# Projections of a decoder layer: tokens normalised ahead of v's eviction, and x1 kept by batches behind keys

## The reference

```python
# x, ctx: (128, 64, 128) = (S, N, D)
x = x + attn(layernorm(x))              # over s for each n: softmax(tanh(q k / sqrt(D))) x, one head
xn = layernorm(x)
q, k, v = xn @ Wq.T + bq, ctx @ Wk.T + bk, ctx @ Wv.T + bv   # over n for each s, 16 heads of 8
x = x + (softmax(q k^T * 8**-0.5) v) @ Wo.T
x = x + soft_moe(x)                     # 16 experts of 16 slots; softmax over tokens and over slots
```

## Time and profile before

| what | value |
|---|---|
| runs | 594.53, 594.87, 598.77 us (median 594.87) |
| the profiled execution | 592.56 us, of which the span on the engines is 590.8 |
| PE busy | 505.0 us (85%) |
| DVE, ACT, POOL busy | 389.9 (66%), 376.9 (64%), 293.8 us (50%) |
| mean share of the 16 DMA engines, SP's queue | 26.5% |
| mean granted TensorE clock | 0.945 |

### The profile page before, as it was taken

One profiled execution on the slowest core, in us unless ns is written; L12 is line 12 of the kernel. 1 busy time (PEld: TensorE's weight loads), 2 busy tenths in 40 slices (PEclk: granted clock), 3 DMA queues, 4 the chain that ended last, 5 costly groups with the idle time before them and its releaser, 6 DMA issues. The chain is left out here.

```text
span 590.8 us, 19858 instructions
## 1 busy us (share of the span) xinstructions
PE 505.0 (85%) x7708; PEld 357.8 (61%) x7708; DVE 389.9 (66%) x1081; ACT 376.9 (64%) x567; POOL 293.8 (50%) x399
## 2 busy tenths in 40 slices
PE   4878858889879999999983089999999976999995
PEld 2557645565346666666652045655655645999995
DVE  4477635769978889899724366666676521677774
ACT  3757824555668878787782358889888654544440
POOL 4234313465668687787402876798898422100000
PEclk9979978999989999999998589999999985999998
DMA  6642114551001110111110002232232231444553
GB/s 183 184 138 107 73 55 137 164 153 46 1 22 35 29 41 25 40 28 36 41 41 1 1 36 75 75 111 94 76 111 96 84 100 48 158 138 146 159 152 98
DMA packets 60737, 49.32 MB, mean 83 GB/s; under 512 B 15472, under 2 KB 50416, under 8 KB 60656
## 3 DMA queue, kind: packets, MB, share of 16 engines
q1 hardware_dynamic: 60656, 48.20, 26.5%
HBM read 30.87 MB, written 17.04 MB: 81 GB/s over the span
## 5 line engine op out<-in xcount | busy, mean ns | idle before, releaser
L587 DVE TENSOR_REDUCE c_mx<-ps 128x16 f32<-128x1024 f32 x64 | 78.0, 1219 | 14.2 <-PE ps L742 13.3
L541 POOL TENSOR_TENSOR c_k_bd<-c_k,w_mask 128x512 bf16<-128x512 f32 x80 | 83.5, 1069 | 1.2 <-DVE c_work L625 1.2
L664 ACT ACTIVATE c_work<-ps 128x2048 f32<-128x2048 f32 x32 | 60.0, 1874 | 27.2 <-PE ps L771 27.1
L1330 PE MATMUL ps<-w_w,h_bd 128*64 128x128 f32 x1024 | 71.8, 280 | 5.5 <-DVE o_slot_out L1282 5.5
L1330 PEld LDWEIGHTS ps<-w_w,h_bd 128*64 128x64 f32 x1024 | 63.5, 141 | 6.3 <-DVE o_slot_out L1282 6.3
L1274 ACT ACTIVATE h_bd<-hidden 32x512 f32 (+1 forms) x64 | 40.3, 629 | 41.1 <-PE ps L1330 40.5
L1306 DVE TENSOR_TENSOR o_slot_out<-ps,w_b 128x512 f32<-128x512 f32 x64 | 44.0, 687 | 21.3 <-PE ps L1330 20.9
L1091 ACT ACTIVATE e_slot_in<-ps 128x1024 f32<-128x1024 f32 x32 | 32.5, 1017 | 27.9 <-PE ps L1153 27.9
L1344 PE MATMUL ps<-o_slot_out,ctx_sb 128*64 128x129 f32 x512 | 41.8, 274 | 1.3 <-DMA ctx_sb<-combine_scratch 0.9
L674 ACT ACTIVATE c_q_bd<-x_all,w_mask 128x512 f32<-128x512 f32 x64 | 42.9, 719 | 0.0
L561 POOL COPY c_v_bd<-c_v 64x512 f32<-64x512 f32 x32 | 21.8, 682 | 35.4 <-PE ps L791 26.8
(11 more groups left out here) (162 smaller groups left out, 1169.3 us busy)
## 6 DMA issues: line engine op xcount, KB each, us to landing
x_all<-x_scratch SPq DMA_DIRECT2D x128, 64.0 KB, 2.3
combine_scratch<-e_comb SPq DMA_DIRECT2D x16, 512.0 KB, 2.7
ctx_sb<-combine_scratch SPq DMA_DIRECT2D x16, 512.0 KB, 3.2
x_sb<-in_x SPq DMA_DIRECT2D x16, 256.0 KB, 3.3
ctx_sb<-in_ctx SPq DMA_DIRECT2D x16, 256.0 KB, 3.2
x_scratch<-a_x SPq DMA_DIRECT2D x16, 256.0 KB, 2.0
e_rden<-dispatch_inverses SPq DMA_DIRECT2D x64, 64.0 KB, 2.0
out<-o_y SPq DMA_DIRECT2D x64, 64.0 KB, 2.1
```

Of the source, the lines that this page charges most:

```text
L541: ins = nc.gpsimd.tensor_tensor(k_bd[:, c.m2, s, :], k32[:, c.v, :], w["mask8"][:, s:s + 1].to_broadcast([P, TOK]), ALU.mult)
L587: nc.vector.reduce_max(mx[:, c.m2, :, p], ps[:, SCORE:SCORE + 2, :].rearrange("p a (h m) -> p (a h) m", m=N), AX_X).then_inc(mx_sb.sem, 1)
L664: nc.scalar.activation(prob[:, h, :], ps[:, 0:4, :].rearrange("p a b -> p (a b)"), ACT.Exp, scale=float(HD) ** -0.5).then_inc(p_sb.sem, 1)
L1330: ins = nc.tensor.matmul(ps[64 * (g % 2):64 * (g % 2) + 64, p, at:at + D], h_bd[:, c.m2, s % 2 * PC + s // 2, g].rearrange("p e k -> p (e ...
```

## The change

1. The scratch tensor x1 is laid out [N, S, D] instead of [S, N, D]. A store of stage 1 now has 512 pieces of 512 B instead of 128 of 2 KB.
2. A chunk's token at half a, column q is now s = 8c + 4a + q, so the four tokens of a partition lie next to each other in DRAM. The load of a chunk (in stage 2, and again in stage 3) is one transfer of 256 KB in 128 pieces of 2 KB instead of four of 64 KB in pieces of 512 B. On the DRAM side it runs over [2 halves][64 n][512 elements], on the SBUF side over [128 partitions][512 elements]. The semaphores count one landing instead of four; `k_at` and the index of `v_bd` follow.
3. DVE normalises chunk t+19 ahead of v(t+20)'s eviction instead of behind it.
4. The output of a chunk goes out by two transfers of 128 KB instead of four of 64 KB.

```diff
+    x1_tokens = x1_dram.rearrange("n s d -> s n d")
-                    sp.dma_start(x1_dram[:, bass.ts(c.v, BC), :], x1[:, c.m2]).then_inc(x1_out.of(c), 16)
+                    sp.dma_start(x1_tokens[:, bass.ts(c.v, BC), :], x1[:, c.m2]).then_inc(x1_out.of(c), 16)
...
-    x1_v = x1_dram.rearrange("(c u a r) n d -> c u a n r d", u=2, a=2, r=2)
+    x1_v = x1_dram.rearrange("n (c a p) d -> c a n (p d)", a=2, p=PC)
...
-                    for u in range(2):
-                        for a in range(2):
-                            sp.dma_start(x_all[N * a:N * (a + 1), c.v * PC + 2 * u:c.v * PC + 2 * u + 2, :], x1_v[c.v, u, a]).then_inc(x_in.of(c), 16)
+                    sp.dma_start(x_all[:, c.v * PC:(c.v + 1) * PC, :].rearrange("p q d -> p (q d)"), x1_v[c.v]).then_inc(x_in.of(c), 16)
...
-                            rows, q_at, k_at = slice(32 * T, 32 * (T + 1)), (4 * u + 2 * r + a) * N, (4 * u + 2 * a + r) * N
+                            rows, q_at, k_at = slice(32 * T, 32 * (T + 1)), (4 * u + 2 * r + a) * N, (4 * a + 2 * u + r) * N
...
-    out_v = out.rearrange("(c u a r) n d -> c u a n r d", u=2, a=2, r=2)
+    out_v = out.rearrange("(c a p) n d -> c a n p d", a=2, p=PC)
...
-                for u in range(2):
-                    for a in range(2):
-                        sp.dma_start(out_v[bass.ds(c.v, 1), u, a].rearrange("o n r d -> (o n) r d"),
-                                     y[N * a:N * (a + 1), c.m2, 2 * u:2 * u + 2, :]).then_inc(y_out.of(c), 16)
+                for a in range(2):
+                    sp.dma_start(out_v[bass.ds(c.v, 1), a].rearrange("o n p d -> (o n) p d"), y[N * a:N * (a + 1), c.m2]).then_inc(y_out.of(c), 16)
...
-        x1_dram = nc.dram_tensor("x1_scratch", [S, N, D], F32).ap()
+        x1_dram = nc.dram_tensor("x1_scratch", [N, S, D], F32).ap()
```

More of the change, by code:

```diff
@@ L463, in cross_attention @@
     zeroed, ps_zeroed, ones_set = kit.sem("c_zeroed"), kit.sem("c_ps_zeroed"), kit.sem("c_ones_set")
-    x_in = kit.landings("c_x_in", 4)
+    x_in = kit.landings("c_x_in")
     stat, rooted, normed = kit.sig("c_stat", 2), kit.sig("c_rooted", 2), kit.sig("c_normed")
@@ L470, in cross_attention @@
     k_bd_dve, k_bd_pool = kit.sig("c_k_bd_dve"), kit.sig("c_k_bd_pool")
-    x_again = kit.pairs("c_x_again", 4)
+    x_again = kit.pairs("c_x_again")
     sc_ps, mx_sb = kit.sig("c_sc_ps", 4), kit.sig("c_mx_sb", 4)
@@ L514, in _ @@
                     sp.wait_ge(q_bd_sb.sem, q_bd_sb.at(c))
-                    for u in range(2):
-                        for a in range(2):
-                            sp.dma_start(x_all[N * a:N * (a + 1), c.v * PC + 2 * u:c.v * PC + 2 * u + 2, :], x1_v[c.v, u, a]).then_inc(x_again.of(c), 16)
+                    sp.dma_start(x_all[:, c.v * PC:(c.v + 1) * PC, :].rearrange("p q d -> p (q d)"), x1_v[c.v]).then_inc(x_again.of(c), 16)
         @block.gpsimd
@@ L612, in _ @@
                     ins.then_inc(stat.sem, 1)
[L613 to L619, removed]
                 c = t.plus(LEAD_X + 2)
@@ L627, in _ @@
                     ins.then_inc(normed.sem, 1)
+                c = t.plus(LEAD_C)
+                if c:
+                    dve.wait_ge(v_ps.sem, v_ps.at(c))
+                    nc.vector.tensor_tensor(
+                        v_all[:, c.v * PC:(c.v + 1) * PC, :], ps[:, MISC, :].rearrange("p (a d) -> p a d", a=PC),
+                        w["bv"][:].rearrange("p (o d) -> p o d", o=1).to_broadcast([P, PC, D]),
+                        ALU.add).then_inc(v_sb.sem, 1)
                 c = t.plus(LEAD_X + 3)
@@ L740, in scores @@
                     for T in range(2):
-                        rows, q_at, k_at = slice(64 * T, 64 * (T + 1)), (4 * u + 2 * r + a) * N, (4 * u + 2 * a + r) * N
+                        rows, q_at, k_at = slice(64 * T, 64 * (T + 1)), (4 * u + 2 * r + a) * N, (4 * a + 2 * u + r) * N
                         ins = nc.tensor.matmul(ps[N * r:N * (r + 1), SCORE + T, :].rearrange("p (s m) -> p s m", s=8),
@@ L790, in values @@
                             to, of = (2 * T + a) * N, (8 * T + 4 * a + j) * N
-                            ins = nc.tensor.matmul(ps[32 * j:32 * j + 2 * V1, VALUE, to:to + N], v_bd[:, c.m2, 2 * u + a, 4 * T + j, :],
+                            ins = nc.tensor.matmul(ps[32 * j:32 * j + 2 * V1, VALUE, to:to + N], v_bd[:, c.m2, 2 * a + u, 4 * T + j, :],
                                                    prob[:, u, of:of + N], start=True, stop=True)
@@ L1239, in experts_out @@
     y_ps, den, y_sb = kit.sig("o_y_ps", 4), kit.sig("o_den", 2), kit.sig("o_y_sb", 2)
-    y_out = kit.landings("o_y_out", 4)
-    out_v = out.rearrange("(c u a r) n d -> c u a n r d", u=2, a=2, r=2)
+    y_out = kit.landings("o_y_out", 2)
+    out_v = out.rearrange("(c a p) n d -> c a n p d", a=2, p=PC)
     first, last, lo, hi = -2, CHUNKS, 2, CHUNKS - 2
```

## The result

The changed kernel takes 623.12 us (median of 4 runs, 621.48 to 626.66) against 594.7 us for the kernel before (4 runs, 593.04 to 598.77). The ratio is 1.047 with a 95% interval of 1.0431 to 1.0509: slower by 28 us. The profiled execution is the longest of its four, 626.66 us with a span of 624.9.

A forecast was written before the change was run, and what follows sets the result against it. Stage 2, bound by a loop through PE and DVE, would become bound by x1's loads on two engines: 592.56 + 32.8 - 0.4 + 1.0 + 0.4 - 1.6 = 624.8, with 1.2 added for typical runs 626 us, range 617 to 637.

The forecast's parts named there:

- Engines per load: Loads of x1: each transfer goes over two engines, because its DRAM side begins with a count of 2.
- sixteen-engine rivals: Loads of x1 get sixteen engines: 586 us with the order's gain, chance 0.13; 592.6 us without it, chance 0.04.
- Price of a load: Stage 2: 5.4 us a load on two engines, 6.3 us a chunk with context; last statistics 32.8 us later.
- Behind the last landing: End of stage 2: DVE's way from last landing to last normalising takes 4.2 us instead of 4.58, -0.4 us.
- The clock: Stage 2: PE's gaps lower its granted clock to 0.50, costing +1.0 us (0 to 3) at the stage's end.
- the rival of 636 us: Stage 2: PE at clock 0.50 becomes the bound with steps of 7.4 us, 636 us in all, chance 0.15.
- Stage 3: Second fetch of x1, also on two engines: 0 us; at worst PE pays 14 us.
- The stores: Stage 1: smaller pieces lengthen DVE's one wait for a store, +0.4 us (0 to 1.5).
- The tail: Output at the kernel's end: two issues a chunk instead of four, -1.6 us (-2.0 to -0.8).
- Part 3, 6.5 us if the tokens come in time: Stage 2: normalising ahead of v's eviction leaves a DVE and POOL loop of 3.4 us, PE's step 3.7, gain 6.5 us.
- the sixteen-engine rival's 586: Loads of x1 on sixteen engines, 0.7 us each, and the new DVE order gives its 6.5 us: 586 us, chance 0.13.
- The third rival: Sixteen engines, but POOL's masks, sharing its queue with the roots, close the loop at 4.2 us: 592.6 us, chance 0.04.

The follow-up runs named there:

- halves: The changed kernel with each load of x1, in stages 2 and 3, sent as two transfers of 64 rows: 591.55 us, ratio 0.9952 to the kernel before.
- cut62: halves with each half load of stage 2 cut into transfers of 62 and 2 rows: 622.93 us, ratio 1.0487 to the kernel before.
- cut61: halves with each half load of stage 2 cut into transfers of 61 and 3 rows: 700.73 us in one run.
- again_by_one: halves with only stage 3's second fetch of x1 put back to one transfer per chunk: 590.44 us, ratio 0.9955 to the kernel before.
- layout_only: The kernel before with x1 kept by batches, its four loads per chunk, DVE order and output unchanged: 595.72 us, ratio 1.0017.
- halves_v_first: halves with v's eviction put back ahead of the normalising on DVE: 593.59 us, ratio 0.9981 to the kernel before.
- before_masks_later: The kernel before with POOL's masks of stage 2 made to wait for the normalising of their step: 598.45 us, ratio 1.0074.
- masks_later: halves with POOL's masks of stage 2 made to wait for the normalising of their step: 587.4 us, ratio 0.9882 to the kernel before.

## Why the prediction was right, and where its terms were off

The kernel is slower, by the mechanism named and within the range of 617 to 637 us. The forecast of 626.0 is 2.9 us above the median. Part of this closeness is luck. Between the two profiled executions there are 34.1 us, of which 30.9 arose up to stage 3, 0.8 in stage 3, 4.6 in stage 4 up to its first L1325, and -2.2 behind. The forecast had 33.8 for the first, nothing for the next two and -1.6 for the last: too much for the loads, nothing for what varies between executions.

- **Engines per load.** Two, as read from the send of the sums. The changed kernel, halves, cut62 and cut61 show it from four sides. The sixteen-engine rivals are out.
- **Price of a load.** This term of the sum was mis-sized: 5.15 us instead of 5.4, and 5.9 to 6.1 a chunk with context instead of 6.3. From the first statistics at 96.64 to the last at 183.97 it is 87.3 us, where the prediction's terms give 15 x 5.4 + 12 x 0.9 = 91.8, 4.5 too much. Two errors went the other way: the first load was issued 1.15 us later (88.07 for 86.92), and DVE had it 8.6 us after its issue, not 6.7. The last statistics were forecast at 185.4 and came at 183.97.
- **Behind the last landing.** 188.14 - 183.97 = 4.17 us; 4.2 was forecast.
- **The clock.** The granted clock was 0.91 in 92 to 137 us and 0.96 behind it, so it did fall behind some of the gaps: from 104 to 106 us, behind a wait of 4.1 us, it was 0.50. But stage 3 starts 30.9 us later than before, exactly as much as the last normalising: the +1.0 at the stage's end did not show, and the rival of 636 us did not come, since PE waits for tokens in all 16 steps. The profiled execution has some 4.6 us more in stage 4 (the first L1325, L1330 before, at 532.1 instead of 495.8, while stage 3 ended 31.7 later). There the windows, before and changed kernel, read:
```profile
335.00:365.00 30.00, 24.55 (x193) 14.45 (x197) 18.61 (x55) 19.39 (x33) 20.43 (x31) 0.84 0.09 36
```
```profile
367.00:397.00 30.00, 24.85 (x154) 14.09 (x155) 15.87 (x47) 17.52 (x31) 19.53 (x27) 0.72 0.09 36
```
  The clock was 0.72 instead of 0.84 in this one execution. The three other runs are 2.7 to 5.2 us shorter, and cut62, with the same stage 2, has the clock at 0.88 there and a span of 619.9. Which of the stages varies from run to run was not followed further.
- **Stage 3.** Forecast at 0. From its first PE instruction for the row of maxima (L764 before) to PE's first of stage 4 (L1192 before) it lasts 173.3 us in the changed kernel and 172.5 before; versions with halves lie between 172.7 and 175.2. again_by_one confirms it.
- **The stores.** +0.4 did not show: 5.0 us of waiting in the changed kernel, 4.5 in layout_only, whose stage 2 begins as before. The changed kernel's later start of stage 2 (88.07) is not the stores' either: halves and cut62 have the same stage 1, and their first loads go out at 86.37 and 86.69. It varies from execution to execution.
- **The tail.** -1.6 forecast, 5.3 - 3.7 = 1.6 measured in the spans; halves_v_first beside the kernel before agrees with 1.4, within noise.
- **Part 3, 6.5 us if the tokens come in time.** This step was wrong. It took no part in the forecast's 626, but it would have made the sixteen-engine rival's 586 wrong: halves is that case, at 591.55. What failed is the sum of DVE's and POOL's loop to 3.4 us. It took the normalising's 1.02 us from a step in which POOL was idle, and moved it to a place where POOL's mask runs. Where no mask ran, in halves up to 105 us, DVE's normalisings do start 3.4 us apart (98.66, 102.07, 105.47); with the mask it is 4.1. The third rival had that place, POOL's masks, and its 592.6 is nearest; its reason, that they share POOL's queue with the roots, was not what the trace shows. POOL stood idle 1.8 us ahead of each root; the masks held DVE instead.

## What to carry to other kernels

Before four transfers are made into one, look at the outermost count of both sides, as the instruction carries it: here 64 against 2 decided between sixteen engines and two, and 62 or 61 rows cost as much or more. A low DMA share beside long waits for DMA was the sign here. When an instruction is moved, look at what the neighbour engine does at its new place: a duration read where POOL was idle is not the duration beside POOL, and a step that should have shrunk to 3.7 us stayed at 4.1 to 4.3 until POOL's mask was moved out of its way.

## What was not expected of the hardware

**DVE beside POOL.** Three times in the timelines above a DVE instruction met POOL's mask of 1.04 us that had begun before it. Each ended as if it had begun 0.8 to 0.9 us after the mask did: in halves 121.62 + 1.06 - 0.34 - 121.55 = 0.79, in before_masks_later 122.78 + 1.20 - 0.45 - 122.66 = 0.87, in masks_later 121.77 + 0.60 - 0.45 - 121.05 = 0.87. POOL's mask lasts 1.04 in all of them. So the second one is held until the first is nearly done; they do not share at half speed. The Trainium skill says this (SBUF — State Buffer, "Who interferes with whom"): the engine that comes first holds the shared pair of ports for the whole instruction, and `tensor_scalar` is among the DVE operations that can want it. The traces agree but for the last 0.2 us of the mask, which no run here settles. The prediction should have used it, and the kernel before already showed it, at the end of stage 2:
```profile
159.78 1.13 DVE L578 TENSOR_SCALAR c_k_bd<-c_k,w_mask 128x512 bf16<-128x512 f32 x1
```
```profile
159.59 1.03 POOL L541 TENSOR_TENSOR c_k_bd<-c_k,w_mask 128x512 bf16<-128x512 f32 x1
```
By the same working 159.78 + 1.13 - 0.45 - 159.59 = 0.87. Not every instruction is held: in masks_later v's eviction at 120.89 and the aggregates at 121.49 lie beside the mask of 121.05 and take their usual 0.68 and 0.37 us.

**SP held by its own issues.** Where the two engines are behind, SP's issue instructions get long. Timeline of SP's queue in the changed kernel:
```profile
107.67 3.64 SPq L503 DMA_DIRECT2D ctx_sb<-in_ctx  x1
111.35 2.23 SPq L499 DMA_DIRECT2D x_all<-x_scratch  x1
113.62 4.19 SPq L503 DMA_DIRECT2D ctx_sb<-in_ctx  x1
```
The pair takes the whole step of 6 us, where in halves two loads take 1.16 us and a context issue 0.37. Context chunks, spread over all sixteen engines, then land 12.8 us after their issue instead of 3.2. The likely reason, which no run tested, is that their share on the two slow engines stands behind the loads. Nobody waits for them here; a kernel with a tighter need on the same queue would pay for that too.
